# Causal attention of a fused image and text kernel: two heads per matmul instead of one

## The reference: what is computed

```python
q = (x @ Wq).reshape(b, n, HEADS, DIM) * DIM ** (-0.5)      # 8 heads of 64
kv_scores, indices = _pk(x, Wq_pk, pk_keys)                 # 16 of 4096 per head
k = einsum('bnhk,bnhkd->bnhd', kv_scores, keys_table[ind])
v = einsum('bnhk,bnhkd->bnhd', kv_scores, values_table[ind])
sim = einsum('bihd,bjhd->bhij', q, k)                       # causal mask, softmax
out = einsum('bhij,bjhd->bihd', attn, v) reshaped @ Wo
```

## Time and profile before

| | |
|---|---|
| median of 3 runs | 8792.01 us (8786.32 to 8822.73) |
| span of the profiled execution, first to last instruction | 12370.4 us |
| busy in it: PE, DVE, ACT, POOL | 7191.2, 5008.5, 3309.2, 5931.2 us |
| mean granted TensorE clock, share of full | 0.566 |
| steady round, in the span | about 742 us |

### The profile page before, as it was taken

How to read it: one execution, slowest core, us unless ns; L and a number is a source line. 1 busy time by engine, 2 the same in 40 slices (tenths; PEclk the granted TensorE clock), 3 DMA queues, 4 the chain that set the end, 5 groups by cost and what they waited for, 6 DMA issues and landing times.

```text
span 12370.4 us, 121689 instructions
## 1 busy us (share of the span) xinstructions
PE 7191.2 (58%) x34736; PEld 5456.4 (44%) x34736; DVE 5008.5 (40%) x16213; ACT 3309.2 (27%) x9869; POOL 5931.2 (48%) x6158
## 2 busy tenths in 40 slices
PE   7758665665756657566665756647576565424103
PEld 5456454443545435454354544435454444313102
DVE  1243625345253442524435253352534435352612
ACT  1112222223222232222322223222222223222222
POOL 0044445455454454544445454454545545565663
PEclk7655655555555555555655555555555555555555
DMA  1011111111111111111111111111111111111111
GB/s 27 7 41 37 35 39 41 38 38 41 36 42 40 40 38 37 41 41 39 36 38 45 36 42 38 37 41 40 39 40 41 39 38 41 41 41 39 41 47 28
DMA packets 658255, 472.33 MB, mean 38 GB/s; under 512 B 557990, under 2 KB 558494, under 8 KB 657183
## 3 DMA queue, kind: packets, MB, share of 16 engines
q0 software_dynamic: 196608, 403.05, 12.7%
q1 hardware_dynamic: 460896, 60.59, 3.1%
HBM read 461.04 MB, written 2.10 MB: 37 GB/s over the span
## 4 chain that ended last, share of the span: by engine, by line
PE 29%; another core or an unknown queue 27%; issue 18%; DVE 16%; DVEq 4%; ACT 4%; SPq 1%; DMA 1%; POOL 0%; ACTq 0%; POOLq 0%
PE MM L438 5%; DVE KV L876 3%; PE PB L1134 2%; PE PB L1107 2%; ACT GATH L869 2%; PE PB L1172 2%; PE PB L1148 1%; PE PB L1162 1%; PE PB L1131 1%; PE MM L390 1%; DVEq L851 1%; DVE I L814 1%; PE MM L453 1%; DVE PF L852 1%
## 5 line engine op out<-in xcount | busy, mean ns | idle before, releaser
L645 POOL DMA_INDIRECT GATH<-in_table,IDX x6144 | 5925.4, 964 | 6313.4 <-DVE KV L876 3824.1
L869 ACT ACTIVATE GATH<-GATH,WT 128x128 f32<-128x128 f32 x6144 | 1907.1, 392 | 237.8 <-issue 236.8
L438 PE MATMUL MM<-SPEC,SW 128*128 128x8 f32 (+1 forms) x8800 | 1259.7, 297 | 863.1 <-issue 420.6
L876 DVE TENSOR_REDUCE KV<-GATH 128x128 f32<-128x2048 f32 x384 | 1391.0, 3622 | 691.7 <-ACT GATH L869 354.1
L438 PEld LDWEIGHTS MM<-SPEC,SW 128*128 128x128 f32 (+1 forms) x8800 | 1266.8, 264 | 864.4 <-issue 862.5
L506 ACT ACTIVATE U<-MM 128x320 f32<-128x320 f32 (+1 forms) x416 | 219.1, 527 | 1882.2 <-remote 988.1
L547 DVE COPY TURN<-TP 80x512 f32<-80x512 f32 (+1 forms) x512 | 347.1, 684 | 925.4 <-remote 391.8
L390 PE MATMUL MM<-F,TURN 128*128 128x80 f32 x2048 | 436.7, 384 | 464.7 <-DVE TURN L547 345.9
L506 ACT ACTIVATE SPEC<-MM 128x160 f32<-128x160 f32 x320 | 96.1, 300 | 2068.2 <-remote 1283.4
L390 PEld LDWEIGHTS MM<-F,TURN 128*128 128x128 f32 x2048 | 404.5, 292 | 535.1 <-issue 278.6
L477 PEld LDWEIGHTS MM<-G,TURN 80*128 80x128 f32 x2048 | 343.5, 240 | 507.1 <-DVE TURN L547 239.0
(11 more groups left out here) (202 smaller groups left out, 11494.3 us busy)
## 6 DMA issues: line engine op xcount, KB each, us to landing
GATH<-in_table,IDX POOLq DMA_INDIRECT x6144
SW<-in_sw SPq DMA_DIRECT2D x1280, 40.0 KB
CONV<-in_cwb SPq DMA_DIRECT2D x128, 4.0 KB
CONV<-in_cwb SPq DMA_DIRECT2D x128, 0.1 KB
U<-in_xT SPq DMA_DIRECT2D x16, 96.0 KB
out<-OUTB SPq DMA_DIRECT2D x16, 96.0 KB
W1E<-in_w SPq DMA_DIRECT2D x1, 520.0 KB
W2E<-in_w SPq DMA_DIRECT2D x1, 512.0 KB
```

What stands on the lines that cost most here:

```text
L438: m = e.matmul(pv[r, :, k, :], SW[r, half, k % HM, w:w + WID * beside], Sv[r, :, c * MODES + k, :], start=True, stop=True)
L645: e.indirect_dma_start(GATH[:, r, k, :], None, table, bass.IndirectOffsetOnAxis(IDX[:, u // H, u % H, k:k + 1], 0)).then_inc(gath[r], 16)
L869: m = e.activation(GATH[:, r, k, :], GATH[:, r, k, :], ACT.Copy, scale=WT[:, u // H, u % H, k:k + 1])
L876: e.tensor_reduce(KV[:, u // H, u % H, :], GATH[:, u % RING, :, :].rearrange("p k d -> p d k"), AX.X, ALU.add).then_inc(S["gather_free"], 1)
```

## The change

The keys and values of two neighbouring heads are put together on 128 partitions. `KV` is laid out by kind first (all keys, then all values), so that a transpose turns the keys, or the values, of two heads. The queries of two heads come from one matmul and are written twice into a larger `Q5`, which now covers all of AREA2: once times a column of the new `PICK` that is 1/8 on partitions 0 to 63 and 0 on the others, and once with the halves exchanged, so that they stand on a block diagonal. One score matmul then serves two heads. `WO5` becomes block diagonal too, zeroed by POOL and loaded in eight pieces, with a buffer of its own; a value matmul serves two heads. The room for this comes from letting the tokenizer's `FHID` share the buffer `TURN`. The diff, cut to its core (left out: one more load in the count, the waits for 11 and 12 zeroed buffers instead of 10 and 11, and the last index of the wait ahead of the scores):

```diff
-BACK = [("kvA", 2, 3), ("kvB", 3, 3), ("q5A", 2, 4), ("q5B", 3, 4), ("vwA", 2, 3), 
+BACK = [("kvA", 2, 3), ("kvB", 3, 3), ("q5A", 2, 2), ("q5B", 3, 2), ("vwA", 2, 3), 
...
-        FHID = sb("FHID", [128, 2, 512])
+        FHID = TURN
...
-W5 = sb("W5", [128, 512]); WQ5 = W5[0:64, :]; WO5 = W5[:, :].rearrange("p (h d) -> p h d", h=H)
+WQ5 = sb("WQ5", [64, 512]); WO5 = sb("WO5", [128, H // 2, 2 * D]); PICK = sb("PICK", [128, 2])
...
-KV = sb("KV", [128, NT3, H, 2 * D])
-Q5 = QT
+KV = sb("KV", [128, NT3, 2, H, D])
+Q5 = AREA2[:, :].rearrange("p (c n s q) -> p c n s q", c=H // 2, n=6, s=2)
...
-            load(WO5[64:128, :, :].rearrange("p a b -> p (a b)"), wo5)
+            for s in range(2):
+                for c in range(H // 2): load(WO5[64 * s:64 * s + 64, c, 64 * s:64 * s + 64], wo5[:, 128 * c + 64 * s:128 * c + 64 * s + 64])
...
-            e.tensor_reduce(KV[:, u // H, u % H, :], GATH[:, u % RING, :, :].rearrange("p k d -> p d k"), AX.X, ALU.add)
+            e.tensor_reduce(KV[:, u // H, :, u % H, :], GATH[:, u % RING, :, :].rearrange("p k (c d) -> p c d k", c=2), AX.X, ALU.add)
...
-            for n in range(4):
-                yield 3.5 + n
+            for n in range(2):
+                yield 4.5 + 2 * n
                 e.wait_ge(*filled("back", i, "q5B", n))
-                e.tensor_scalar(Q5[:, 2 * n + 1, :], PB[3][0:64, 0:TOK], D ** -0.5, None, ALU.mult).then_inc(empt["back", 3], 1)
+                for s in range(2):
+                    ins = e.tensor_scalar(Q5[:, 2 * n + 1, :, s, :], PB[3][:, 0:TOK].rearrange("p (n q) -> p n q", n=6), PICK[:, s:s + 1], None, ALU.mult)
+                ins.then_inc(empt["back", 3], 1)
...
-            for n in range(4):
-                yield 3.5 + n
+            for n in range(2):
+                yield 4.3 + 2 * n
                 e.wait_ge(*filled("back", i, "q5A", n))
-                e.activation(Q5[:, 2 * n, :], PB[2][0:64, 0:TOK], ACT.Copy, scale=D ** -0.5).then_inc(empt["back", 2], 1)
+                for s in range(2):
+                    ins = e.activation(Q5[:, 2 * n, :, s, :], PB[2][:, 0:TOK].rearrange("p (n q) -> p n q", n=6), ACT.Copy, scale=PICK[:, s:s + 1])
+                ins.then_inc(empt["back", 2], 1)
...
-                    m = e.transpose(PB[2 + n % 2][:, 128 * h:128 * h + 128], KV[:, t, 4 * hh + h, :], ID[:, :])
+                    m = e.transpose(PB[2 + n % 2][:, 128 * h:128 * h + 128], KV[:, t, hh, 2 * h:2 * h + 2, :], ID[:, :])
...
-            for n in range(8):
-                yield 3 + n // 2
+            for n in range(4):
+                yield 3 + n
...
-                e.matmul(PB[2 + n % 2][0:64, 0:TOK], WQ5[:, 64 * n:64 * n + 64], NTC[:, :], start=True, stop=True)
+                e.matmul(PB[2 + n % 2][:, 0:TOK], WQ5[:, 128 * n:128 * n + 128], NTC[:, :], start=True, stop=True)
...
-                for h in range(H):
-                    m = e.matmul(PB[2][:, 64 * h:64 * h + 64], KVT[64:128, h, 128 * t:128 * t + 128], WO5[64:128, h, :], start=True, stop=True)
+                for c in range(H // 2):
+                    m = e.matmul(PB[2][:, 128 * c:128 * c + 128], KVT[:, H // 2 + c, 128 * t:128 * t + 128], WO5[:, c, :], start=True, stop=True)
...
-                    for h2 in range(2):
-                        h = 2 * (2 * half + a) + h2
-                        m = e.matmul(PB[2 + half][64 * h2:64 * h2 + 64, SEQ * a:SEQ * a + jn], Q5[:, h, SEQ * b + 64 * ib:SEQ * b + 64 * ib + 64], KVT[0:64, h, SEQ * b:SEQ * b + jn], start=True, stop=True)
+                    c = 2 * half + a
+                    m = e.matmul(PB[2 + half][:, SEQ * a:SEQ * a + jn], Q5[:, c, 3 * b + ib, :, :], KVT[:, c, SEQ * b:SEQ * b + jn], start=True, stop=True)
...
-                for t in (FW0, FW1, FW2, CONV, KB, ONES, RS, OHS, AREA4, SW):
+                for t in (FW0, FW1, FW2, CONV, KB, ONES, RS, OHS, AREA4, SW, WO5):
...
+                e.memset(PICK[:, :], 0.0); e.drain(); e.memset(PICK[0:64, 0:1], D ** -0.5); e.memset(PICK[64:128, 1:2], D ** -0.5)
```

More of the change, by code:

```diff
@@ L239, in early_fusion @@
         WQ = sb("WQ", [64, H * D]); WK = sb("WK", [64, D]); WV = sb("WV", [64, D]); WOT = sb("WOT", [128, 4, D])
-        WPK = sb("WPK", [64, 512]); KB = sb("KB", [128, 4, 256]); W5 = sb("W5", [128, 512]); WQ5 = W5[0:64, :]; WO5 = W5[:, :].rearrange("p (h d) -> p h d", h=H)
+        WPK = sb("WPK", [64, 512]); KB = sb("KB", [128, 4, 256]); WQ5 = sb("WQ5", [64, 512]); WO5 = sb("WO5", [128, H // 2, 2 * D]); PICK = sb("PICK", [128, 2])
         ID = sb("IDB", [128, 128]); TRI = sb("TRI", [128, 128]); ONES = sb("ONES", [128, 128])
@@ L262, in early_fusion @@
         XC = sb("XC", [128, NT3, D]); NTC = NT2[0:64, :]
-        GATH = sb("GATH", [128, RING, TOPK, 2 * D]); KV = sb("KV", [128, NT3, H, 2 * D])
-        Q5 = QT; KVT = sb("KVT", [128, H, TOK]); VW = AREA3[:, :].rearrange("p (t h d) -> p t h d", t=NT3, h=H)
+        GATH = sb("GATH", [128, RING, TOPK, 2 * D]); KV = sb("KV", [128, NT3, 2, H, D])
+        Q5 = AREA2[:, :].rearrange("p (c n s q) -> p c n s q", c=H // 2, n=6, s=2); KVT = sb("KVT", [128, H, TOK]); VW = AREA3[:, :].rearrange("p (t h d) -> p t h d", t=NT3, h=H)
         P5 = AREA1[:, 3072:4608].rearrange("p (s h t) -> p s h t", s=2, h=4); NM5 = sb("NM5", [128, 2, 4]); DEN5 = sb("DEN5", [128, 2, 4]); PT = AREA4[:, :].rearrange("p (s n) -> p s n", s=3)
@@ L587, in sp_setup @@
             e.sem_inc(row_out, 16)
-            e.wait_ge(zeroed, 10)
+            e.wait_ge(zeroed, 11)
             def load(d, s, **k):
@@ L617, in sp_mixers @@
             assert n[0] == NLOADS, n[0]
-        NLOADS = 1 + 2 + 14 + 2 + 16
+        NLOADS = 1 + 2 + 14 + 1 + 8 + 16
         def sp_front(e, j, g):
@@ L1241, in t_back @@
                 fence(e)
-                e.matmul(PB[2 + n % 2][0:64, 0:TOK], WQ5[:, 64 * n:64 * n + 64], NTC[:, :], start=True, stop=True).then_inc(full["back", 2 + n % 2], 1)
+                e.matmul(PB[2 + n % 2][:, 0:TOK], WQ5[:, 128 * n:128 * n + 128], NTC[:, :], start=True, stop=True).then_inc(full["back", 2 + n % 2], 1)
             yield 7
@@ L1283, in outs @@
                 m.then_inc(full["back", 1], 1)
-            e.wait_ge(*emptied("back", i, "q5A", 3)); e.wait_ge(*emptied("back", i, "q5B", 3))
+            e.wait_ge(*emptied("back", i, "q5A", 1)); e.wait_ge(*emptied("back", i, "q5B", 1))
             yield 10
@@ L1376, in before @@
                 e.sem_inc(tp_out, CREDIT); e.sem_inc(tp_full, CREDIT)
-                e.memset(NTR[64:65, :], 1.0); e.memset(NEG[:, :], -FMAX); e.memset(BIG[:, 0:1], 1e4); e.memset(BIG[:, 1:2], -1e4)
+                e.memset(NTR[64:65, :], 1.0); e.memset(NEG[:, :], -FMAX); e.memset(PICK[:, :], 0.0); e.drain(); e.memset(PICK[0:64, 0:1], D ** -0.5); e.memset(PICK[64:128, 1:2], D ** -0.5); e.memset(BIG[:, 0:1], 1e4); e.memset(BIG[:, 1:2], -1e4)
                 e.wait_ge(tokenizer_in, 16 * N_TOKENIZER)
@@ L1390, in before @@
                 e.sem_inc(mm_out, CREDIT); e.sem_inc(mm_full, CREDIT)
-                e.wait_ge(tokenizer_in, 16 * N_TOKENIZER); e.wait_ge(zeroed, 10)
+                e.wait_ge(tokenizer_in, 16 * N_TOKENIZER); e.wait_ge(zeroed, 11)
             def mixers(e):
-                e.wait_ge(const_in, 16 * NLOADS); e.wait_ge(zeroed, 11)
+                e.wait_ge(const_in, 16 * NLOADS); e.wait_ge(zeroed, 12)
             before(e)
```

2 lines of the change are left out of this document (1 added, 1 removed).

## The result

The changed kernel takes 8744.0 us (median of 4 runs, 8737.11 to 8753.74), the kernel before 8800.32 us in the same comparison (4 runs, 8786.32 to 8822.73): a ratio of 0.9938, 95% interval 0.9917 to 0.9959. That is 56 us or 0.62% faster; the interval goes from 0.41 to 0.83%. The forecast was 72 us less, 0.82%, with 8720.

The account below looks back on a forecast made before the run. DVE and ACT lines were taken to lead the loop's attention part, PE the last, lone attention. PE's -170 us at 0.4 gave -68, with -10 for banks and +6 for evictions and start: -72, 8720 us, range 8610 to 8815.

Parts of the forecast that it names:

- The standstills: Stretches of the profile where PE, DVE and ACT stand still while POOL's gathers run; taken to belong mostly to that execution.
- Value weights: Output weights applied to the values (L1250): 24 matmuls per pair become 12, saving 82 us of PE.
- Scores: Score matmuls (L1260): 48 per pair become 24 over the full array; only 64-column groups change, dearer by 28 us of PE.
- Queries: Query matmuls (L1242): 8 per pair become 4 with 64x128 weights; half of 151.8 us busy, saving 76 us of PE.
- Borders: On PE, rows overlap more where full-array work follows full-array work: at most 40 us saved.
- PE together: Sum of the expected changes to PE's instruction time: -170 us, 10.6 us per pair.
- Evictions: Writing the query products out on DVE and ACT, scaled by a column of PICK: +4 us for both engines together.
- Handed-back banks: PE waits less at the query matmuls, each bank being returned once instead of three times per pair: -10 us.
- The share on the path: Part of PE's 170 us saving that would shorten the kernel: 0.4, giving -68 us.
- (a): Rival: DVE and the gathers set the loop's top-k and attention part, PE only waits longer; 8790 us, chance 0.28.
- (b): Rival: PE bounds the timed runs and each us saved counts; -170 to -270 us, some 8580, chance 0.08.
- (c): Rival: shorter PE trains no longer raise the granted clock where the attention ends; +126 us, 8846, chance 0.12.

Follow-up runs that it names:

- the second profile: The kernel before, unchanged, profiled once more: the run took 8823.22 us and its profile spans 8821.4 us.
- 12 of 16 rows: Both kernels fetching 12 instead of 16 table rows per gather unit: kernel before 8495.15 us (0.9635), changed kernel 8418.17 us (0.9556).

## Why the prediction was right, and where it was not

**The standstills** belonged to the profiled execution: the second profile has none. But "busy times of instructions carry over" did not hold for PE, 7191.2 against 6795.3 us: in the standstills the granted clock was at 0.50. This hit one term, the queries.

**Value weights**, -82 us: -81.6, and a tile in 2.05 us, near the 1.97 of L407's row. **Scores**, +28: +23.9. By the Trainium skill's page "TensorEngine Tiling (Array Packing)", section Key Properties, different tiles of the array can load weights and multiply in parallel, and by that rule alone no width would have got dearer. The trace nearly agrees at 128 and 192 columns (1.97 against 2.04 us, 2.83 against 2.93) and does not at 64 (1.12 against 1.94), where the row decided rightly. **Queries**, -76: -54.6, because 76 was half of the slow profile's 151.8, and because a group of two records takes 0.6 and not half of the time of four.

**Borders**, -40: this did not come. The overlap of rows of different lines grew by 5 us. What the lines that the change leaves alone lost, 102.5 us, is mostly records that ran at the upper clock level instead of the lower one, a gain that no term of the sum had. **PE together**, -170: -220, of which the terms of the sum make 112 and 5; that the total is not far off is luck.

**Evictions**, +4 for both engines: L906 36.1 against 34.5 us and L1017 33.2 against 30.2, together +4.6. One of them became dearer by more than the bound of 0.05 us (538 to 607 ns on DVE, 472 to 571 on ACT), but two in a row overlap. **Handed-back banks**, -10: nothing is shown for it. PE's wait for DVE's L904 was 10.0 us and is 12.6 for L906; what fell in front of the queries is mainly one long wait late in the program. **The reduce**, 0: 3627 against 3629 ns. **The start**: the first L438 begins at 63.63 us after and 63.83 before, so the eight loads and the memset stayed hidden.

**The share on the path**, 0.4, is the step that failed in part. In the loop 73 of 191 us arrived, 0.38, with and without the shorter gathers; but 0.4 was read from the shares of a chain with standstills in it and meant for the change's own terms, and of the 191 us only 82 are that. Undoing the value weights gives 0.4 for their own 82 us, with a wide error. It failed in the last three pairs, which the sum treated like all others: PE's 22 us there bring nothing, because 384 gathers in a row, each 1.25 us after the one before (last section), take 480 us a pair, and 1450.6 us are three times 484. Over the whole program 56 of 220 us arrived by the medians, 0.25 us for a us (75 by the two profiles, 0.34). A PE sum that the clock made larger and a smaller share nearly cancelled, which is why 8720 came close; the parts did not, and the closeness is luck.

**The rivals.** (a), hidden by DVE and the gathers, is what happens to six tenths of what PE lost in the loop and to all of it in the last pairs. In the last pairs it is the gathers, as shown. In the loop PE waits longer for DVE (the 126 us above), and the gathers stand close behind. That DVE's busy time is the bound of the second parts (206 of 227 us) is not shown: with 22 us less of it they were no shorter. It may be the fixed order in which the engines wait for each other; the run that would tell, less work on DVE with shorter gathers, was not made. (b), PE as the bound, fell: 56 of 220 us arrived, and the 82 us that came back with the value weights cost 33. The chain by itself would have supported it, since it gives PE 51% before; what it does not tell is how closely the next engine stands behind. (c), the clock falling, fell: it rose, from 0.604 to 0.616 in the profiles, and took 55 us off PE's work in four lines alone. By the Trainium skill's page "TensorE: Matmul & The Clock Gate" (Part 1), activity releases the throttle and its lack brings it back. Here PE had fewer instructions (33456 against 34736) and was granted more, so that no throttle came back for a cut of this size.

**What would show it.** L1255 near 1.97 (2.05), score groups no shorter, the clock within 0.03 and the last back 5 us shorter (7) came out. So did most of the rest showing as PE waiting for DVE: 126 of 144 us more of idle time, though in front of the tokenizer's matmuls and not of the queries. The queries at half their busy time (0.60 of it) and busy PE down by 130 to 170 us (220) did not.

## What to carry to other kernels

Price a saving by stretch: here the same cut on one engine was worth 0.38 us a us in the loop and nothing in the last rounds. Before reading such a rate off busy times, split them into the lines that the change touches and the others: a good part of what PE lost here was a higher clock on work that had not changed. An engine's share of the chain says what waits now and not how far behind the next engine stands; shorten that engine's work, as with 12 of 16 rows, before counting on the next us. Before packing two small matmuls into one with zeros, look whether they already run side by side in the trace: here the packing paid where it halved the instructions of one position (value weights, queries), not where two positions were in use (scores).
